# Moving an output projection's matmuls from the score part of each step into its softmax part

## The chip, the core and the metric

The kernel runs on one core of one Trainium2 chip. The metric is the device time of one execution in microseconds. Before the change it is 1201.21 us, the median of 3 runs (1199.9 to 1201.53).

The names used below: PE is the matrix engine (TensorE), DVE the vector engine, ACT the scalar engine, POOL is GpSimd, SP the engine whose queue issues most DMAs. Each engine runs its own instruction stream in order; they meet only at semaphores.

## The reference

One transformer block on `x` of 16 x 256 x 512 in float32: banded cross attention with rotary positions against a context of the same shape, then a quantised feed-forward layer.

```python
B, window = 128, 128                       # dk = 32, 16 heads
qp = _rope(einsum('bsd,ed->bse', layernorm(x), wq)); kp = _rope(einsum(..., ctx, wk)); vp = einsum(..., ctx, wv)
scores = einsum('bhnqd,bhnkd->bhnqk', qb, kband) * sqrt(dk)      # band of +-128 keys, rest masked
out = einsum('bhnqk,bhnkd->bhnqd', softmax(scores), vband)
x = x + (einsum('bsd,ed->bse', out, wo_w) + wo_b)
hidden = gelu(quantize_a16(layernorm(x)) @ quantize_w8(W_in) + b_in)
x = x + (quantize_a16(hidden) @ quantize_w8(W_out) + b_out)
```

## The kernel before, in words

The program has an attention phase (up to about 735 us of the span) and a feed-forward phase behind it. The change touches only the attention phase. It takes the 16 sequences one after the other, one step `b` for each sequence of 256 tokens, all 16 heads in a step. Matrix products whose operands need float32 accuracy are made of three products in the fp32r type: each operand is split into a leading part (`_hi`) and a rest (`_lo`), and hi x hi, hi x lo and lo x hi are summed.

A step is pipelined over three sequences. In step b the engines do the attention of sequence b, the projections (k, q, v) of sequence b + 1, and the output projection (`o_products`, with `wo`), residual and second layernorm's moments of sequence b - 1. Step 0 has no output projection (`has_o` is false), step 15 no projections (`has_proj` is false); steps 1 to 14 have both.

PE's order within a step is written out by hand in `step`:

- The score part. `scores(b, n)` makes the 256 x 256 scores of head n as two matmuls of 256 columns, into one of two banks of PSUM in turn (`ring`). DVE adds the mask and takes the row maxima (`row_maxima`, L1218, two instructions for a head); `scores` of head n may start only when the maxima of head n - 2 are done. Between the heads stand the projections of the next sequence: `tiles[n]` holds what PE does behind the scores of head n. The v projection of the second token half is 12 matmuls of 512 columns (`v_tile(b + 1, 1)`), 9 of them behind head 11 and 3 behind head 12.
- DVE's `split_max` (L1223 and L1225) then makes the negated maxima in two parts. PE transposes them (`max_transposes`, L617), ACT copies them into the stacked operand `q_st` (`max_copy`, L960), and SP spreads them to the other heads by three DMAs (`stack_max`, L352).
- The softmax part. `scores_t(b, n)` (L639) makes the transposed scores of head n with the maximum already subtracted, into three banks in turn; ACT takes the exponential (L967), POOL cuts the band (`band`, L1559). Behind heads 7, 11 and 15, and at the end, a `clump` of 32 narrow matmuls weighs v and sums the denominators of four heads.

The output projection of sequence b - 1 is 24 matmuls of 512 columns, 12 for each token half s, into `kv_bank[s]`. `o_products` is a generator: each `some(count)` in `step` issues the next `count` of them. Before the change 2 are issued behind head 14, 10 behind the last scores, 4 behind the transposes and 8 between the transposed scores. Within a half the 8 products with `t_hi` come first and the 4 with `t_lo` last, and the wait for `ot_lo` stands ahead of the latter. `t_hi` (ACT, `ot_lead`, L944) and `t_lo` (POOL, `ot_rest`, L1547) are the two parts of the normalised attention output; ACT's comes first, behind DVE's `normalise` (L1265), which stands behind head 9.

POOL's order in a step is: `split_lo` for k (L1536, four instructions), `ot_rest` twice, `bias_x` (L1552: adds the output bias to the residual's input `x_res`, two instructions, behind a wait for the DMA that loads `x_res`), then the first two quarters of `ctx_lo` (L1542), then the bands. DVE's `residual` (L1211) waits for the finished half (`o_mm`) and for `bias_x`. SP issues the load of `x_res` at the start of a step; in step 15 it first issues the loads of two tiles of the feed-forward phase's input (`load_xq`, 1 MB each).

## Time and profile before

| | |
|---|---|
| median of 3 runs | 1201.21 us |
| the profiled execution | 1201.21 us |
| its span, first to last instruction | 1199.5 us |
| PE busy | 1147.4 us (96%) |
| DVE busy | 953.4 us (79%) |
| ACT busy | 643.3 us (54%) |
| POOL busy | 373.3 us (31%) |
| granted PE clock, mean over the span | 0.987 |

The profiled execution took exactly the median, and 1.7 us of it lie outside the span. A busy PE is not a PE at its peak: its records overlap (the end of a matmul is modelled and lies behind the start of the next), so how fast PE goes is read from the distance between starts. In the timeline, "x4" is four merged instructions, and a bracket gives the engine's idle time before the row and what released it. The granted clock is 1.00 at 2.4 GHz and 0.50 at 1.2 GHz.

### The profile page before, as it was taken

To read this page: it belongs to the slowest core of one execution; us is meant where nothing else is said; L and a number is where in the kernel's file an instruction comes from. 1 tells how busy PE (TensorE), PEld (TensorE's weight loads), DVE (VectorE), ACT (ScalarE), POOL (GpSimd) and SP (SyncE) were. 2 spreads that over 40 slices of the span, in tenths; PEclk is the share of its full clock that TensorE was granted. 3 is DMA by queue.
4 is the path that set the end of the run, shared out by engine and by line. 5 is a ranking of instruction groups with operands and counts; after the bars stand their busy time and mean duration, and the time that the engine had idled before them with its cause. 6 is when DMAs were issued, how large, how long until landed. Compare 5 with 4: busy or idle time off the path is not lost.

```text
span 1199.5 us, 23540 instructions
## 1 busy us (share of the span) xinstructions
PE 1147.4 (96%) x7928; PEld 766.8 (64%) x7928; DVE 953.4 (79%) x2413; ACT 643.3 (54%) x1033; POOL 373.3 (31%) x540
## 2 busy tenths in 40 slices
PE   6989999999999999999999788999999999999998
PEld 6867877887787787788778555444444444444443
DVE  6769889989888988998898766666666688777776
ACT  6244355346435535634543454565655468777774
POOL 1146337436534733743563330000000021111121
PEclk9989999999999999999999889999999999999999
DMA  8454674574566458356545732555553402577662
GB/s 287 117 139 108 177 196 104 160 202 131 130 181 171 110 161 215 90 165 192 144 117 145 191 113 88 194 192 194 205 191 138 158 1 71 177 240 236 223 220 97
DMA packets 100522, 191.10 MB, mean 159 GB/s; under 512 B 13376, under 2 KB 30912, under 8 KB 100416
## 3 DMA queue, kind: packets, MB, share of 16 engines
q1 hardware_dynamic: 96096, 179.92, 49.7%
q10 hardware_dynamic: 4320, 9.83, 2.9%
q8 instruction: 59, 0.97, 0.3%
q14 instruction: 47, 0.39, 0.1%
HBM read 89.16 MB, written 43.91 MB: 111 GB/s over the span
## 4 chain that ended last, share of the span: by engine, by line
PE 47%; issue 24%; DVE 20%; DMA 5%; ACT 2%; SPq 1%; DVEq 0%; POOL 0%; POOLq 0%; ACTq 0%
PE bank L858 18%; DVE bank L1218 9%; PE bank L653 5%; PE bank L639 5%; PE bank L666 4%; DMA q_st<-q_st 3%; PE bank L515 3%; PE bank L514 3%; PE bank L516 3%; DVE row_max L1218 2%; PE bank L605 2%; DVE roped L1244 2%; DVE rt L1242 2%; DVE neg_max L1223 1%; DVE rt L1241 1%
## 5 line engine op out<-in xcount | busy, mean ns | idle before, releaser
L1218 DVE CUSTOM_DVE_ANT_0 bank<-bank,mask 128x256 f32<-128x256 f32 x512 | 202.7, 454 | 54.1 <-PE bank L605 44.5
L858 PE MATMUL bank<-wout_int,g_hi 128*128 128x512 bf16 x512 | 193.6, 379 | 0.1
L858 PE MATMUL bank<-wout_int,g_lo 128*128 128x512 bf16 x512 | 193.6, 379 | 0.0
L819 PE MATMUL bank<-qT_hi,win_int 128*128 128x512 bf16 x496 | 188.0, 379 | 0.0
L819 PE MATMUL bank<-qT_lo,win_int 128*128 128x512 bf16 x496 | 188.0, 379 | 0.0
L967 ACT ACTIVATE probs<-bank 128x512 f32<-128x512 f32 x256 | 135.7, 602 | 40.4 <-PE bank L639 38.8
L1536 POOL TENSOR_TENSOR k_lo<-roped,k_hi 128x256 fp32r<-128x256 f32 x60 | 55.2, 948 | 284.7 <-ACT k_hi L907 284.7
L1514 DVE TENSOR_TENSOR g_lo<-h_int,g_hi 128x512 f16<-128x512 f32 x128 | 89.1, 696 | 41.3 <-ACT g_hi L1123 37.4
L1559 POOL TENSOR_SCALAR_AFFINE_SELECT probs<-probs 128x256 f32<-128x256 f32 x256 | 107.0, 428 | 46.8 <-ACT probs L967 39.5
L639 PE MATMUL bank<-q_st,k_st 128*128 128x256 f32 x512 | 103.6, 302 | 11.4 <-DMA q_st<-q_st 6.0
L639 PEld LDWEIGHTS bank<-q_st,k_st 128*128 128x128 f32 x512 | 82.9, 192 | 44.4 <-issue 13.6
L1091 ACT ACTIVATE h_ring<-bank,b_in,g_scale 128x512 f32<-128x512 f32 x96 | 72.9, 778 | 71.4 <-PE bank L819 55.0
L1456 DVE TENSOR_REDUCE hmax<-h_ring 128x512 f32 (+1 forms) x96 | 63.1, 682 | 58.2 <-ACT h_ring L1091 56.3
L605 PE MATMUL bank<-k_st,q_st 96*128 96x256 f32 x512 | 96.8, 301 | 11.3 <-DVE row_max L1218 10.4
L1123 ACT CAST g_hi<-h_int 128x512 f16<-128x512 f32 x128 | 78.9, 617 | 47.2 <-PE bank L858 43.2
L605 PEld LDWEIGHTS bank<-k_st,q_st 96*128 96x128 f32 x512 | 77.5, 194 | 34.0 <-DVE row_max L1218 16.8
L1602 POOL TENSOR_TENSOR xq<-xq,b_out 128x512 f32<-128x512 f32 x32 | 41.5, 1296 | 166.5 <-ACT h_int L1132 166.5
L858 PEld LDWEIGHTS bank<-wout_int,g_hi 128*128 128x128 f16 x512 | 50.0, 98 | 60.9 <-issue 0.6
L858 PEld LDWEIGHTS bank<-wout_int,g_lo 128*128 128x128 f16 x512 | 50.1, 98 | 60.3 <-DVE g_lo L1514 0.2
L819 PEld LDWEIGHTS bank<-qT_hi,win_int 128*128 128x128 bf16 x496 | 48.5, 98 | 57.8 <-ACT h_ring L1091 0.3
L819 PEld LDWEIGHTS bank<-qT_lo,win_int 128*128 128x128 bf16 x496 | 48.5, 98 | 57.7
L1132 ACT ACTIVATE h_int<-h_ring,magic_c,tiny 128x512 f32<-128x512 f32 x96 | 77.9, 812 | 0.0
(170 smaller groups left out, 2678.4 us busy)
## 6 DMA issues: line engine op xcount, KB each, us to landing
hidden_scratch<-h_ring SPq DMA_DIRECT2D x96, 256.0 KB, 2.1
h_ring<-hidden_scratch SPq DMA_DIRECT2D x96, 256.0 KB, 2.8
k_st<-k_hi SPq DMA_DIRECT2D x128, 128.0 KB, 2.6
q_st<-q_hi SPq DMA_DIRECT2D x128, 128.0 KB, 2.6
xq<-x_scratch SPq DMA_DIRECT2D x16, 1024.0 KB, 6.1
x_ln<-in_x SPq DMA_DIRECT2D x16, 512.0 KB, 6.4
ctx_raw<-in_ctxT SPq DMA_DIRECT2D x16, 512.0 KB, 5.1
k_st<-k_lo SPq DMA_DIRECT2D x64, 128.0 KB, 2.7
```

The costliest lines, as they stand in the source:

```text
L605: mm = pe.matmul(ring[n % 2][:, qb * S:(qb + 1) * S], q_st[0:MROW, n, qb * P:(qb + 1) * P], k_st[0:MROW, n], start=True, stop=True)
L639: mm = pe.matmul(third[n][:, kb * S:(kb + 1) * S], k_st[:, n, kb * P:(kb + 1) * P], q_st[:, n], start=True, stop=True)
L819: mm = pe.matmul(bank[f % 4][:], win_int[:, c, f * P:(f + 1) * P], part[:, par, c], start=c == 0 and part is qT_hi, stop=c == KC - 1 and p ...
L858: return pe.matmul(bank[4 * par + u][:], part[:, f % 4, u * P:(u + 1) * P], wout_int[:, f], start=f == 0 and part is g_hi, stop=f == FC - ...
L967: act.activation(probs[:, n % SLOTS].rearrange("p k q -> p (k q)"), third[n][:], ACT.Exp, scale=SCORE_SCALE).then_inc(exp_done, 1)
L1091: act.activation(dst, bank[f % 4][:], ACT.Gelu, bias=b_in[:, f:f + 1], scale=g_scale[:, f:f + 1]).then_inc(gelu_done, 1)
L1123: act.copy(g_hi[:, f % 4], h_int[:, f % 4]).then_inc(ghi_done, 1)
L1132: act.activation(h_int[:, f % 4], chunk, ACT.Identity, bias=magic_c[:], scale=tiny[:, 5:6]).then_inc(hint_done, 1)
L1218: dve.tensor_tensor_reduce(sc, sc, mask[:, (1 - qb) * P:(1 - qb) * P + S], 1.0, NEG, ALU.add, ALU.max, row_max[:, qb, n:n + 1]).then_inc(m ...
L1456: dve.tensor_reduce(hmax[:, bass.ds(FC * n + f, 1)], src, AX_X, ALU.max, apply_absolute_value=True).then_inc(hmax_done, 1)
L1514: dve.tensor_tensor(g_lo[:, f % 4], h_int[:, f % 4], g_hi[:, f % 4], ALU.subtract).then_inc(glo_done, 1)
L1559: pool.affine_select(out=far, in_=far, compare_op=ALU.is_ge, fill=0.0, base=1 - P, pattern=[[0, 2], [1, P]], channel_multiplier=1).then_in ...
```

## The change

PE's o products of a step now stand 4 ahead of the transposes (10 + 2 before), 4 behind them (as before) and 16 between the transposed scores (8 before). Each product triple goes hi x hi, hi x lo, lo x hi within one chunk, so the wait for `ot_lo` of a half now stands ahead of its first product. The v projection's second half is cut 6 + 6, behind heads 11 and 13, instead of 9 + 3 behind heads 11 and 12. On POOL, `bias_x` stands ahead of `ot_rest`.

```diff
--- before.py
+++ after.py
@@ -575,6 +575,7 @@
                 for s in range(2):
                     tok = slice(s * P, (s + 1) * P)
                     pe.wait_ge(ot_hi, 2 * j + s + 1)
+                    pe.wait_ge(ot_lo, 2 * j + s + 1)
                     if s == 0:
                         pe.wait_ge(w_lo_done, 5)
                     if has_proj:
@@ -582,15 +583,13 @@
                     else:
                         pe.wait_ge(res_done, 2 * j)
                     for c in range(KC):
-                        for w in (w_hi, w_lo):
-                            pe.matmul(kv_bank[s][:], t_hi[:, c, tok], w["wo"][:, c], start=c == 0 and w is w_hi, stop=False)
+                        parts = ((t_hi, "hi"), (t_hi, "lo"), (t_lo, "hi"))
+                        for m, (part, w) in enumerate(parts):
+                            mm = pe.matmul(kv_bank[s][:], part[:, c, tok], (w_hi if w == "hi" else w_lo)["wo"][:, c],
+                                           start=c == 0 and m == 0, stop=c == KC - 1 and m == 2)
+                            if c == KC - 1 and m == 2:
+                                mm.then_inc(o_mm, 1)
                             yield
-                    pe.wait_ge(ot_lo, 2 * j + s + 1)
-                    for c in range(KC):
-                        mm = pe.matmul(kv_bank[s][:], t_lo[:, c, tok], w_hi["wo"][:, c], start=False, stop=c == KC - 1)
-                        if c == KC - 1:
-                            mm.then_inc(o_mm, 1)
-                        yield
 
             def scores(b, n):
 
@@ -718,32 +717,32 @@
 
             def step(b, par, has_c, has_o, has_proj, has_xt):
 
-                tiles = [[] for _ in range(H)]
+                tiles = [[] for _ in range(H // 2)]
+                if has_proj:
+                    tiles[0] += [lambda: qk_tile(b + 1, "k", 0)]
+                    tiles[1] += [lambda: x_transposes(b + 1, 0), lambda: x_transposes(b + 1, 1), lambda: qk_tile(b + 1, "k", 1)]
+                    tiles[2] += [lambda: v_tile(b + 1, 0)]
+                    tiles[3] += [lambda: qk_tile(b + 1, "q", 0)]
+                    tiles[4] += [lambda: qk_tile(b + 1, "q", 1)]
+                    tiles[5] += [lambda: v_tile(b + 1, 1, range(2))]
+                    tiles[6] += [lambda: v_tile(b + 1, 1, range(2, KC))]
+                for n in range(H):
+                    scores(b, n)
+                    if n % 2:
+                        for tile in tiles[n // 2]:
+                            tile()
+
+
                 heavy = o_products(b - 1, has_proj) if has_o else iter(())
 
                 def some(count):
                     for _ in range(count):
                         next(heavy, None)
 
-                if has_proj:
-                    tiles[1] += [lambda: qk_tile(b + 1, "k", 0)]
-                    tiles[3] += [lambda: x_transposes(b + 1, 0), lambda: x_transposes(b + 1, 1), lambda: qk_tile(b + 1, "k", 1)]
-                    tiles[5] += [lambda: v_tile(b + 1, 0)]
-                    tiles[7] += [lambda: qk_tile(b + 1, "q", 0)]
-                    tiles[9] += [lambda: qk_tile(b + 1, "q", 1)]
-                    tiles[11] += [lambda: v_tile(b + 1, 1, range(3))]
-                    tiles[12] += [lambda: v_tile(b + 1, 1, range(3, KC))]
-                tiles[14] += [lambda: some(2)]
-                for n in range(H):
-                    scores(b, n)
-                    for tile in tiles[n]:
-                        tile()
-
-
-                some(10)
+                some(4)
                 max_transposes(b, has_proj)
                 some(4)
-                for n, count in enumerate((1, 1, 1, 1, 1, 1, 1, 0, 1, 0, 0, 0, 0, 0, 0, 0)):
+                for n, count in enumerate((1, 2, 2, 3, 1, 1, 1, 0, 1, 1, 1, 0, 1, 1, 0, 0)):
                     scores_t(b, n, has_o, has_proj)
                     some(count)
                     if n in (7, 11, 15):
@@ -1569,9 +1568,10 @@
                     for c in range(KC):
                         split_lo("k", b + 1, c)
                 if has_o:
+                    bias_x(b - 1)
+                if has_o:
                     ot_rest(b - 1, 0)
                     ot_rest(b - 1, 1)
-                    bias_x(b - 1)
                 if has_xt:
                     ctx_lo(b + 2, 0)
                     ctx_lo(b + 2, 1)
```

The places on PE and POOL in step 1 (steps 2 to 14 are alike). First PE's tail of the score part. L605 (L604 after) are the scores, two matmuls for a head; L514 to L516 the v projection; L586 and L590 (L588 after) the o products; L617 (L616 after) the transposes of the maxima. Before, from the scores of head 12 on, where the two heads 13 and 14 are one row of four:

```order
L605 MATMUL bank<-k_st,q_st 128x256 x2
L514 MATMUL bank<-wv_hi,cT_hi 128x512
L515 MATMUL bank<-wv_lo,cT_hi 128x512
L516 MATMUL bank<-wv_hi,cT_lo 128x512
L605 MATMUL bank<-k_st,q_st 128x256 x4
L586 MATMUL bank<-wo_hi,t_hi 128x512
L586 MATMUL bank<-wo_lo,t_hi 128x512
L605 MATMUL bank<-k_st,q_st 128x256 x2
```

After, from the six v matmuls that now stand behind head 13 (the first row is heads 12 and 13, the last heads 14 and 15):

```order
L604 MATMUL bank<-k_st,q_st 128x256 x4
L514 MATMUL bank<-wv_hi,cT_hi 128x512
L515 MATMUL bank<-wv_lo,cT_hi 128x512
L516 MATMUL bank<-wv_hi,cT_lo 128x512
L514 MATMUL bank<-wv_hi,cT_hi 128x512
L515 MATMUL bank<-wv_lo,cT_hi 128x512
L516 MATMUL bank<-wv_hi,cT_lo 128x512
L604 MATMUL bank<-k_st,q_st 128x256 x4
```

Three of the nine v matmuls behind head 11 have moved behind head 13, and the two o products between heads 14 and 15 are gone.

PE ahead of the transposes, before, from the last scores on:

```order
L605 MATMUL bank<-k_st,q_st 128x256 x2
L586 MATMUL bank<-wo_hi,t_hi 128x512
L586 MATMUL bank<-wo_lo,t_hi 128x512
L586 MATMUL bank<-wo_hi,t_hi 128x512
L586 MATMUL bank<-wo_lo,t_hi 128x512
L586 MATMUL bank<-wo_hi,t_hi 128x512
L586 MATMUL bank<-wo_lo,t_hi 128x512
L590 MATMUL bank<-wo_hi,t_lo 128x512 x4
L617 MATMUL bank<-ident,neg_max 128x128 x2
```

After:

```order
L604 MATMUL bank<-k_st,q_st 128x256 x4
L588 MATMUL bank<-wo_hi,t_hi 128x512
L588 MATMUL bank<-wo_lo,t_hi 128x512
L588 MATMUL bank<-wo_hi,t_lo 128x512
L588 MATMUL bank<-wo_hi,t_hi 128x512
L616 MATMUL bank<-ident,neg_max 128x128 x2
```

Ten products between the last scores and the transposes have become four, and the third of the four already reads `t_lo`.

PE between the transposed scores of heads 0 to 4, before (L639 are the transposed scores):

```order
L639 MATMUL bank<-q_st,k_st 128x256 x2
L586 MATMUL bank<-wo_hi,t_hi 128x512
L639 MATMUL bank<-q_st,k_st 128x256 x2
L586 MATMUL bank<-wo_lo,t_hi 128x512
L639 MATMUL bank<-q_st,k_st 128x256 x2
L586 MATMUL bank<-wo_hi,t_hi 128x512
L639 MATMUL bank<-q_st,k_st 128x256 x2
L586 MATMUL bank<-wo_lo,t_hi 128x512
L639 MATMUL bank<-q_st,k_st 128x256 x2
```

After (L638 are the transposed scores):

```order
L638 MATMUL bank<-q_st,k_st 128x256 x2
L588 MATMUL bank<-wo_hi,t_lo 128x512
L638 MATMUL bank<-q_st,k_st 128x256 x2
L588 MATMUL bank<-wo_hi,t_hi 128x512
L588 MATMUL bank<-wo_lo,t_hi 128x512
L638 MATMUL bank<-q_st,k_st 128x256 x2
L588 MATMUL bank<-wo_hi,t_lo 128x512
L588 MATMUL bank<-wo_hi,t_hi 128x512
L638 MATMUL bank<-q_st,k_st 128x256 x2
L588 MATMUL bank<-wo_lo,t_hi 128x512
L588 MATMUL bank<-wo_hi,t_lo 128x512
L588 MATMUL bank<-wo_hi,t_hi 128x512
```

Eight products stand here instead of four. Four more have moved behind heads 8 to 13.

POOL in step 1, before:

```order
L1536 TENSOR_TENSOR k_lo<-roped,k_hi 128x256 x4
L1547 TENSOR_TENSOR t_lo<-oT,t_hi 128x4x128 x2
L1552 TENSOR_TENSOR x_res<-x_res,wo_b 128x512 x2
L1542 TENSOR_TENSOR cT_lo<-ctx_raw,cT_hi 128x256 x2
L1559 AFFINE_SELECT probs<-probs 128x256 x2
```

After:

```order
L1535 TENSOR_TENSOR k_lo<-roped,k_hi 128x256 x4
L1551 TENSOR_TENSOR x_res<-x_res,wo_b 128x512 x2
L1546 TENSOR_TENSOR t_lo<-oT,t_hi 128x4x128 x2
L1541 TENSOR_TENSOR cT_lo<-ctx_raw,cT_hi 128x256 x2
L1558 AFFINE_SELECT probs<-probs 128x256 x2
```

The two instructions that write `x_res` and the two that write `t_lo` have changed places.

## Rows read from the trace of the kernel before

**Rows 1.** List of waits, whole span: engine, line waited for, total us, times, longest
```profile
PE bank L617 <- DVE neg_max L1225: 10.5, 15, 1.6
```

**Rows 2.** Timeline, PE, end of a steady step's score part: start us, us, instruction
```profile
313.95 0.40 PE L605 MATMUL bank<-k_st,q_st 96*128 96x256 f32 x2
...
314.89 0.40 PE L605 MATMUL bank<-k_st,q_st 96*128 96x256 f32 x2
315.56 0.51 PE L605 MATMUL bank<-k_st,q_st 96*128 96x256 f32 x2 [0.27 <-DVE row_max L1218]
...
316.41 0.50 PE L605 MATMUL bank<-k_st,q_st 96*128 96x256 f32 x2
...
318.14 1.09 PE L590 MATMUL bank<-wo_hi,t_lo 128*128 128x512 f32 x4
319.91 0.44 PE L617 MATMUL bank<-ident,neg_max 128*128 128x128 f32 x2 [0.68 <-DVE neg_max L1225]
...
320.89 0.40 PE L586 MATMUL bank<-wo_lo,t_hi 128*128 128x512 f32 x1
321.13 0.39 PE L639 MATMUL bank<-q_st,k_st 128*128 128x256 f32 x2
```

**Rows 3.** Timeline, DVE, the same stretch
```profile
313.49 0.13 DVE L1218 DVE_READ_ACCUMULATOR2_ANT row_max<- 128x1 f32 x1
...
314.54 0.43 DVE L1218 CUSTOM_DVE_ANT_0 bank<-bank,mask 128x256 f32<-128x256 f32 x1
...
318.01 1.15 DVE L1223 TENSOR_SCALAR neg_max<-row_max 128x32 fp32r<-128x32 f32 x1
319.20 0.66 DVE L1225 SCALAR_TENSOR_TENSOR neg_max<-row_max,neg_max 128x32 fp32r<-128x32 f32 x1
```

**Rows 4.** Timeline, POOL, the same stretch
```profile
314.10 2.54 POOL L1547 TENSOR_TENSOR t_lo<-oT,t_hi 128x512 fp32r<-128x512 f32 x2
316.61 2.52 POOL L1552 TENSOR_TENSOR x_res<-x_res,wo_b 128x512 f32<-128x512 f32 x2
319.09 1.41 POOL L1542 TENSOR_TENSOR cT_lo<-ctx_raw,cT_hi 128x256 fp32r<-128x256 f32 x2
```

**Rows 5.** One line's instructions, L1223 and L1225: ns min/median/max, first and last start
```profile
L1223 DVE TENSOR_SCALAR neg_max<-row_max x16: 181/1172/1187, 61.0 to 695.7; 128x32 fp32r<-128x32 f32 x16
...
L1225 DVE SCALAR_TENSOR_TENSOR neg_max<-row_max,neg_max x16: 192/656/658, 61.2 to 695.9; 128x32 fp32r<-128x32 f32 x16
```

**Rows 6.** Timeline, PE, the same step's transposed part and the next step's start
```profile
323.46 0.51 PE L639 MATMUL bank<-q_st,k_st 128*128 128x256 f32 x2 [0.30 <-DMA q_st<-q_st]
...
325.30 1.07 PE L653 MATMUL bank<-probs,v_sb 128*32 128x256 f32 x16
...
327.17 0.51 PE L639 MATMUL bank<-q_st,k_st 128*128 128x256 f32 x2
...
331.85 0.50 PE L639 MATMUL bank<-q_st,k_st 128*128 128x256 f32 x2 [0.22 <-ACT probs L967]
...
336.34 0.74 PE L605 MATMUL bank<-k_st,q_st 96*128 96x256 f32 x4
```

**Rows 7.** Timeline, PE, the last step (15): its first row and its transposes
```profile
676.06 0.74 PE L605 MATMUL bank<-k_st,q_st 96*128 96x256 f32 x4
...
697.84 0.38 PE L617 MATMUL bank<-ident,neg_max 128*128 128x128 f32 x2
```

**Rows 8.** Timeline, POOL, the last step
```profile
690.43 2.50 POOL L1547 TENSOR_TENSOR t_lo<-oT,t_hi 128x512 fp32r<-128x512 f32 x2 [16.88 <-ACT t_hi L944]
696.58 2.53 POOL L1552 TENSOR_TENSOR x_res<-x_res,wo_b 128x512 f32<-128x512 f32 x2 [3.65 <-DMA x_res<-in_x]
```

**Rows 9.** Busy time by stretch: length, busy of each engine, granted clock, DMA
```profile
58.50:61.90 3.40, 1.37 (x6) 0.72 (x6) 3.33 (x16) 1.07 (x3) 1.41 (x2) 1.00 0.00 0
61.97:72.00 10.03, 8.03 (x48) 5.09 (x48) 8.16 (x17) 6.07 (x11) 6.55 (x12) 0.50 0.52 119
318.00:321.40 3.40, 2.72 (x15) 1.90 (x14) 3.32 (x5) 1.01 (x2) 2.50 (x3) 1.00 0.00 0
```

## The prediction

> **What bounds the kernel now.** I read the busy shares first: PE is busy 96% of the span, DVE 79%. Then the list of waits, for what stops PE in the attention phase: the transposes of the maxima wait for DVE's L1225 in 15 of the 16 steps [rows 1]. Then the timelines of one steady step, engine by engine, where the change sits. The scores of heads 0 and 1 of the next step start at 336.34, those of step 15 at 676.06, eight steps later [rows 6, 7]: a steady step takes (676.06 - 336.34) / 8 = 42.5 us.
>
> In that step PE has two regimes. From the scores of head 12 at 313.95 to the transposes at 319.91 it follows DVE: head 14 waits 0.27 us for the maxima of head 12, and behind the last o product of the twelve PE waits again 0.68 us, for L1225 [rows 2]. From the transposed scores at 321.13 to the next step's scores at 336.34 it is 15.21 us of nearly dense work, with stops that are small: 0.30 for the DMA that spreads the maxima, 0.22 for an exponential [rows 2, 6].
>
> What ends the first regime is not DVE's arithmetic. L1223 takes 0.18 us in its shortest case and 1.17 in the median; L1225 0.19 and 0.66 [rows 5]. In the steady step L1223 starts at 318.01 and ends at 319.16, and POOL's fourth instruction of the rest and bias pairs ends at 316.61 + 2.52 = 319.13; L1225 then ends at 319.86, and the first of POOL's two `ctx_lo` instructions ends near 319.09 + 1.41 / 2 = 319.8 [rows 3, 4]. So each of them lasts until the POOL instruction that it met is over, and the transposes' time is set by POOL's row of work.
>
> **The v projection's cut, 6 + 6.** A 512 column product is 0.24 us from start to start (320.89 to 321.13) [rows 2]. Three fewer ahead of head 12 let its scores start up to 0.7 us sooner, at 313.25, but they need the maxima of head 10, which DVE has at 313.49 + 0.13 = 313.62 [rows 2, 3]; they start near 313.68. Head 13 then waits for the maxima of head 11, near 314.4. Behind it stand six v matmuls instead of two score heads: 314.44 + 0.34 (the longer start after a wait, 315.56 to the next matmul) + 6 x 0.235 = 316.2 for head 14, 0.6 later than the 315.56 of before; head 15 follows at 316.4, as before. DVE got to head 12 0.59 us behind its scores (313.95 to 314.54) and needs 0.77 for a head, so its last maxima end near 318.3 instead of 317.9, 0.4 later. L1223 then starts at 318.4, still within the POOL instruction that ends at 319.13, and ends when it did. I take 0 for the cut. If L1223's length were its own, it would be +0.4 a step, 14 x 0.4 = 5.6 us.
>
> The Trainium skill, in GPSIMD Engine Reference (Specifications), says that GpSimd's SBUF interfaces are shared with VectorE, with contention for DVE instructions in a two-port mode or with two SBUF inputs. By it L1225, with two inputs in SBUF, is such a one, and the 0.4 is swallowed; by the instruction's duration alone 5.6 us would be added. The trace agrees with the page (0.18 against 1.17 us).
>
> **The wait for `ot_lo` and POOL's new order.** The four instructions are 1.27 and 1.26 us each and only change places [rows 4]: bias to 316.61, rest of half 0 to 317.9, of half 1 to 319.13. PE's first o product needs half 0 now: with the last scores out at 316.7 it stops until 317.9, does four products (until 319.0) and stops again until 319.91. Queued behind the first stop are these four and the transposes, which aren't ready anyway. 0 us.
>
> **Eight o products moved behind the transposes.** This is the term. Before, ten stood between the last scores and the transposes and two between heads 14 and 15; of those twelve four remain. PE's idle time ahead of the transposes grows by what they were, 8 x 0.235 = 1.9 us, and they come back in the dense part. Walked through: from 321.13 to the transposed scores of head 4 stand 4 heads and 8 products, 12 x 0.235 = 2.8, so 323.95 instead of 323.46, since the DMA's 0.30 stop and the slower start behind it go: +0.5 for four more products. To the first clump three heads with products and one without, as before, without the start after a stop: +0.4 there (325.30 before). The second quarter had 1.62 us (327.17 to the next clump) with one product and a stop for exponentials; three products fit into 0.1 + 7 x 0.235 = 1.7: +0.1. The third quarter has two more products but its 0.22 stop goes, and its head 15 waits for the exponential of head 12 whatever stands between: 0 [rows 6]. Sum 0.45 a step, and 14 x 0.45 = 6.3 us. The ends: all stops of before swallow it (0), or none do (14 x 1.9 = 26 us); I stay with the walk, because its stops are in the rows. DVE's residual of half 0 comes at 323.9, half 0's last product at 322.8; half 1's is done near 332.4, the residual at 332.9: no new wait, with 0.5 us to spare.
>
> **Step 0** has no o products; the score cut lets DVE end about 0.4 us sooner, with POOL idle: -0.4 us.
>
> **Step 15.** Here the swap on POOL costs. `t_lo` was made at 690.43 to 692.9, and `bias_x` started only at 696.58, when the load of `x_res` had landed behind two loads of 1 MB [rows 8]. With the bias ahead, `t_lo` of half 0 comes at 696.58 + 2.53 + 1.26 = 700.4, and PE, in order, has its four products and then the transposes behind that wait. PE runs at half clock there (it has been idle most of the step), so the four take 4 x 0.47 = 1.9 us, and the transposes are at 702.3 instead of 697.84 [rows 7]: +4.4. The products behind them start at half clock too, some 4 of them, +0.9; the extra ones behind head 8 vanish between exponentials. Taken +5.5. The bounds: if `x_res` lands ahead of 690, the step gains some 1.5 us (six products fewer ahead of transposes whose maxima are ready); if the half clock lasts through the step's softmax part, +9.
>
> **The clock.** The granted clock fell to 0.50 (1.2 GHz) in step 0, behind 3.4 us in which PE was busy 1.37, and stayed there 10 us; in the steady step, with 2.72 of 3.4 us busy across the transposes, it stayed at 1.00 [rows 9]. After the change PE stands idle 1.1 + 0.8 us around four products there, so it is busy about 1.5 of 3.4. That is nearer to the stretch that fell. But step 0 had a sparse softmax part behind it, and here the work behind is dense, so a fall should last some 3.4 us rather than 10 and cost half of that, 1.6 us with the stops gone. No row shows how many steps would fall: between 0 and 14, so 0 to 22 us. I take two, +3, nearer to the row of 1.00 in every steady step, because the average of PE's work over a step hardly moves.
>
> The Trainium skill, in TensorE: Matmul & The Clock Gate (A second HAM failure mode), says that micro-idles between groups of matmuls can make the clock swing between its two levels. By it all 14 steps are in danger; the row of step 0 agrees that a fall behind a sparse stretch happens here, and no row shows it within a steady step.
>
> **The sum.** 1201.2 + 6.3 - 0.4 + 5.5 + 3 = 1215.6, so 1216 us. It starts from the profiled execution's 1201.21, which is the median. A measurement of this kernel tells about 0.2% (2.4 us) from no change.
>
> **The rivals.**
>
> 1. The clock falls in most steady steps. For it: 1.5 of 3.4 us busy is close to the 1.37 that fell. Against it: the dense work on both sides. 14 x 1.6 = 22 instead of 3: 1235 us; with half the steps 1224.
> 2. Only the dense term and a small step 15. For it: step 15's `x_res` is one DMA, with a landing time that could differ by some us, and the clock may not fall. 1201.2 + 6.3 - 0.4 + 0 to 2: 1207 to 1209 us.
> 3. The softmax part swallows all: if ACT's exponentials and not PE set its pace, the eight products cost nothing, as PE's stops there for ACT and the DMA add up with the slow starts behind them to about 1.5 of the 1.9 us; with step 15's gain or loss of up to 2, 1200 to 1203 us: no change. Against it: two of three clumps start behind dense PE rows.
> 4. Faster. ACT makes `cT_hi` only behind the copy of the later v half, so POOL's `ctx_lo` could start later than 319.13. Then L1225 meets an idle POOL and takes 0.19 instead of 0.66, and the transposes come 0.47 sooner in 13 steps: -6.1 us. It decides if `cT_hi` is over 1 us later than I reckon (318.1, the v half 1.3 us later than before). With the softmax part swallowing the products and step 15 at -1.5, 1201.2 - 6.1 - 0.4 - 1.5 = 1193 us; with the dense term it comes out at 1199 and without step 15's gain at no change. It needs three things that I reckon otherwise.
> 5. DVE is later than reckoned and misses POOL's fourth instruction, meeting both `ctx_lo` ones: +0.7 in 13 steps, 1225 us. It has 0.7 us to spare.
>
> **How the numbers follow.** The forecast (two or so falls, step 15 at 4 to 7): 0.45, with 1211 to 1221 as its own range. Rival 1: 0.15. Rival 2: 0.15. Rival 3: 0.10. Rival 4: 0.06. Rival 5: 0.09. The range 1205 to 1229 leaves out rivals 3 and 4 and the upper end of rival 1, together about 0.2. Faster by over 0.2%: 0.05 (most of rival 4). Within 0.2%: 0.10. Slower by over 0.2%: 0.85.
>
> **What would show it.** In a steady step: L1223 still over 0.7 us long and ending with a POOL instruction; the transposes still 5.9 to 6 us behind 313.95's place in the step; PE idle about 1.1 us until POOL's `t_lo` and 0.8 us until L1225; the distance between steps 42.9 instead of 42.5 where the clock is 1.00; the stop for the DMA ahead of head 4 gone. In step 15: PE waiting for POOL's `t_lo`, which stands behind the load of `x_res`, to about 700 plus the shift. The granted clock across the transposes tells rival 1 from the rest. The forecast is wrong if the step distance stays at 42.5, if a steady step stands at 0.50 in most steps, or if step 15's `x_res` lands before its `t_hi`.

## The result and the profile after

| | before | after |
|---|---|---|
| median | 1200.92 us (4 runs, 1199.9 to 1201.53) | 1221.79 us (4 runs, 1219.11 to 1223.11) |
| the profiled execution | 1201.21 us | 1221.89 us |
| its span | 1199.5 us | 1220.0 us |
| PE busy | 1147.4 us | 1146.5 us |
| granted PE clock, mean | 0.987 | 0.977 |

The change makes the kernel slower: the ratio is 1.0172 [1.0152, 1.0192], 20.5 us more in the span. The forecast was 1216, with 1205 to 1229 as its range.

Two distances cut every step of the trace at the same places. The score part runs from the first scores to the transposes of the maxima, the softmax part from these to the next step's first scores. Before, they are 26.1 and 16.4 us in each steady step (steps 1 to 14; the score part of step 14 is 25.6, before and after). After, the score part is 26.05. The softmax part is 17.01 to 17.03 in seven steps (1, 2, 7, 8, 9, 13, 14) and 18.44 to 18.56 in the other seven (3 to 6, 10 to 12).

PE's timeline in step 9, one of the first kind, answers to [rows 2, 6]:

```profile
452.11 0.63 PE L604 MATMUL bank<-k_st,q_st 96*128 96x256 f32 x4
453.84 0.47 PE L588 MATMUL bank<-wo_hi,t_hi 128*128 128x512 f32 x1 [1.09 <-issue]
...
455.78 0.44 PE L616 MATMUL bank<-ident,neg_max 128*128 128x128 f32 x2 [0.77 <-DVE neg_max L1224]
...
459.80 0.39 PE L638 MATMUL bank<-q_st,k_st 128*128 128x256 f32 x2
...
461.52 1.07 PE L652 MATMUL bank<-probs,v_sb 128*32 128x256 f32 x16
...
463.39 0.51 PE L638 MATMUL bank<-q_st,k_st 128*128 128x256 f32 x2
...
465.25 1.07 PE L652 MATMUL bank<-probs,v_sb 128*32 128x256 f32 x16
...
472.79 0.74 PE L604 MATMUL bank<-k_st,q_st 96*128 96x256 f32 x4
```

The two idle stretches around the four o products are there, 1.09 and 0.77 us. The first is put down to "issue", but it ends with POOL's first rest, 452.47 + 1.26 = 453.73 in the next fence. From the transposes the transposed scores of head 4 are 459.80 - 455.78 = 4.02 us away (3.55 before), the first clump 5.74 (5.39), the second 9.47 (8.88), the next step 17.01 (16.43). The stop of 0.30 for the DMA ahead of head 4 is gone.

DVE and then POOL in the same step, answering to [rows 3, 4]:

```profile
454.37 0.66 DVE L1222 TENSOR_SCALAR neg_max<-row_max 128x32 fp32r<-128x32 f32 x1
455.06 0.66 DVE L1224 SCALAR_TENSOR_TENSOR neg_max<-row_max,neg_max 128x32 fp32r<-128x32 f32 x1
```

```profile
449.99 2.52 POOL L1551 TENSOR_TENSOR x_res<-x_res,wo_b 128x512 f32<-128x512 f32 x2
452.47 2.52 POOL L1546 TENSOR_TENSOR t_lo<-oT,t_hi 128x512 fp32r<-128x512 f32 x2
454.96 1.41 POOL L1541 TENSOR_TENSOR cT_lo<-ctx_raw,cT_hi 128x256 fp32r<-128x256 f32 x2
```

DVE's last maxima end 1.41 us ahead of the transposes instead of 1.90 (319.91 - 318.01), so DVE is 0.49 later. L1222 (L1223 before) nevertheless ends where POOL's fourth instruction does, 455.03 against 454.99: it is only shorter, 0.66 instead of 1.15.

Now step 6, one of the seven long ones. PE's timeline:

```profile
323.19 0.47 PE L588 MATMUL bank<-wo_hi,t_hi 128*128 128x512 f32 x1 [1.11 <-issue]
...
325.13 0.69 PE L616 MATMUL bank<-ident,neg_max 128*128 128x128 f32 x2 [0.77 <-DVE neg_max L1224]
325.47 0.78 PE L588 MATMUL bank<-wo_lo,t_hi 128*128 128x512 f32 x1
326.05 0.63 PE L588 MATMUL bank<-wo_hi,t_lo 128*128 128x512 f32 x1
326.47 0.63 PE L588 MATMUL bank<-wo_hi,t_hi 128*128 128x512 f32 x1
```

And busy time by stretch (length, busy time of each engine with its instructions, granted clock, DMA), for step 9, step 6 twice, and step 0 twice; it answers to [rows 9]:

```profile
454.00:457.40 3.40, 2.63 (x13) 1.85 (x13) 3.30 (x7) 1.06 (x2) 2.37 (x3) 1.00 0.00 0
323.30:326.70 3.40, 2.63 (x9) 1.92 (x10) 3.30 (x7) 0.84 (x2) 2.41 (x3) 0.74 0.00 0
325.50:328.20 2.70, 2.70 (x10) 2.22 (x9) 2.63 (x5) 1.27 (x3) 0.21 (x1) 0.50 0.13 31
61.97:68.50 6.53, 5.66 (x29) 4.31 (x32) 6.00 (x12) 5.59 (x11) 4.10 (x9) 0.51 0.52 120
68.50:79.00 10.50, 10.07 (x141) 5.74 (x132) 4.13 (x11) 6.01 (x15) 6.82 (x14) 0.98 0.53 118
```

Steps 6 and 9 have the same instructions and the same idle time. In step 6 the granted clock is 0.50 (1.2 GHz) from the transposes to 328.3 (the row below), the products come 0.42 to 0.43 us apart instead of 0.235, and the softmax part is 1.4 us longer. In step 0 the clock is back at about 68.9 instead of 72.2.

```profile
324.91:328.32 3.41, 3.19 (x10) 2.71 (x11) 3.34 (x6) 1.39 (x3) 0.80 (x2) 0.50 0.14 32
```

In step 15 POOL and then PE answer to [rows 8] and [rows 7]:

```profile
711.20 2.48 POOL L1551 TENSOR_TENSOR x_res<-x_res,wo_b 128x512 f32<-128x512 f32 x2 [21.60 <-DMA x_res<-in_x]
713.65 2.49 POOL L1546 TENSOR_TENSOR t_lo<-oT,t_hi 128x512 fp32r<-128x512 f32 x2
```

```profile
708.20 1.56 PE L604 MATMUL bank<-k_st,q_st 96*128 96x256 f32 x4 [0.42 <-DVE row_max L1217]
715.00 0.76 PE L588 MATMUL bank<-wo_hi,t_hi 128*128 128x512 f32 x1 [5.24 <-issue]
...
716.85 0.63 PE L616 MATMUL bank<-ident,neg_max 128*128 128x128 f32 x2
```

PE stands idle for 5.24 us until `t_lo`, which stands behind the load of `x_res`. The score part of step 15 is 24.74 us instead of 21.78.

The account of the 20.5 us of span, by these distances: the softmax parts without a fallen clock 14 x 0.58 = 8.1; the seven falls of the clock 7 x 1.51 = 10.6 (by their mean softmax part, 18.52 against 17.01); the score parts -0.5; step 0 -2.1 (score part +0.2, softmax part 17.54 instead of 19.85); step 15 +3.0 up to the transposes and +2.2 behind them; the rest, -0.8, lies in the feed-forward phase (-0.7) and in rounding.

### The profile page after: what moved, and what is told of

It reads as the page before. It is cut to its first block, busy times and chain, and to the rows that moved or that the text cites. A ratio compares the mean times of both kernels' runs of the same rounds, so it can differ in the third digit from the quotient of the medians.

```text
span 1220.0 us, 23511 instructions
## 1 busy us (share of the span) xinstructions
PE 1146.5 (94%) x7884; PEld 775.4 (64%) x7928; DVE 946.9 (78%) x2413; ACT 646.5 (53%) x1033; POOL 372.9 (31%) x540
## 4 chain that ended last, share of the span: by engine, by line
PE 55%; issue 24%; DVE 17%; DMA 2%; SPq 1%; ACT 1%; DVEq 0%; POOL 0%; POOLq 0%
PE bank L857 18%; DVE bank L1217 7%; PE bank L588 7%; PE bank L638 6%; PE bank L652 5%; PE bank L665 4%; PE bank L604 3%; PE bank L514 3%; PE bank L515 3%; PE bank L516 3%; DVE row_max L1217 2%; DVE roped L1243 2%; DVE rt L1241 1%; DVE rt L1240 1%; PE bank L529 1%
## 5 line engine op out<-in xcount | busy, mean ns | idle before, releaser
L857 PE MATMUL bank<-wout_int,g_hi 128*128 128x512 bf16 x491 | 185.8, 379 | 0.3 <-issue 0.2
L818 PE MATMUL bank<-qT_hi,win_int 128*128 128x512 bf16 x474 | 179.6, 379 | 0.0
L966 ACT ACTIVATE probs<-bank 128x512 f32<-128x512 f32 x256 | 139.9, 600 | 53.2 <-PE bank L638 49.7
L638 PEld LDWEIGHTS bank<-q_st,k_st 128*128 128x128 f32 x512 | 95.8, 201 | 30.5 <-issue 13.2
L638 PE MATMUL bank<-q_st,k_st 128*128 128x256 f32 x512 | 107.3, 301 | 2.0 <-ACT probs L966 1.1
L604 PE MATMUL bank<-k_st,q_st 96*128 96x256 f32 x512 | 94.0, 300 | 15.8 <-DVE row_max L1217 14.8
L604 PEld LDWEIGHTS bank<-k_st,q_st 96*128 96x128 f32 x512 | 75.3, 194 | 37.1 <-issue 23.4
L947 ACT COPY v_sb<-bank 128x512 f32<-128x512 f32 x32 | 18.8, 586 | 121.2 <-PE bank L516 121.2
```

What stands on the lines that cost most here:

```text
L604: mm = pe.matmul(ring[n % 2][:, qb * S:(qb + 1) * S], q_st[0:MROW, n, qb * P:(qb + 1) * P], k_st[0:MROW, n], start=True, stop=True)
L638: mm = pe.matmul(third[n][:, kb * S:(kb + 1) * S], k_st[:, n, kb * P:(kb + 1) * P], q_st[:, n], start=True, stop=True)
L818: mm = pe.matmul(bank[f % 4][:], win_int[:, c, f * P:(f + 1) * P], part[:, par, c], start=c == 0 and part is qT_hi, stop=c == KC - 1 and p ...
L857: return pe.matmul(bank[4 * par + u][:], part[:, f % 4, u * P:(u + 1) * P], wout_int[:, f], start=f == 0 and part is g_hi, stop=f == FC - ...
L966: act.activation(probs[:, n % SLOTS].rearrange("p k q -> p (k q)"), third[n][:], ACT.Exp, scale=SCORE_SCALE).then_inc(exp_done, 1)
```

## The experiments

Theory A: the loss is three terms, the moved products (some 8 us), falls of the granted clock behind the sparse stretch (some 10), and step 15's swap on POOL (some 5). Theory B: one term, the sparse stretch or the swap, makes nearly all of it. Ratios are against runs of the kernel before on the same chip.

### POOL's order alone (pool_swap)

```diff
                 if has_o:
+                    bias_x(b - 1)
                     ot_rest(b - 1, 0)
                     ot_rest(b - 1, 1)
-                    bias_x(b - 1)
```

> The kernel before with POOL's order alone changed: bias_x ahead of ot_rest. Theory (the swap costs only in the last step): steady steps stay 42.5 us apart, the granted clock stays at 1.00 in them, and in step 15 the transposes come about 5 us later, since POOL's t_lo stands behind the load of x_res: 1206 us (+5). Rival (the swap also delays t_lo in every step, and the o products with it): t_lo of half 0 comes at the place of 317.9 instead of 315.4, and if the first half's lo products then wait, the transposes move by 0.3 us in 14 steps: 1210. Rival (the swap costs nothing): 1201.

Measured: 1204.86 us, ratio 1.0032 [1.0018, 1.0046]. The steady parts are 26.1 and 16.4 as before, in all but step 11, whose softmax part is 17.73. That is no fall, the clock is 1.00 there: ahead of head 4 PE waits for the DMA that spreads the maxima, 1.60 us instead of 0.30.

```profile
536.85 0.50 PE L639 MATMUL bank<-q_st,k_st 128*128 128x256 f32 x2 [1.60 <-DMA q_st<-q_st]
```

Step 15's score part is 26.18 instead of 21.78, +4.4. POOL and then PE there:

```profile
697.36 2.48 POOL L1552 TENSOR_TENSOR x_res<-x_res,wo_b 128x512 f32<-128x512 f32 x2 [23.06 <-DMA x_res<-in_x]
699.80 2.49 POOL L1547 TENSOR_TENSOR t_lo<-oT,t_hi 128x512 fp32r<-128x512 f32 x2
```

```profile
701.12 2.07 PE L590 MATMUL bank<-wo_hi,t_lo 128*128 128x512 f32 x4 [4.27 <-POOL t_lo L1547]
702.99 0.63 PE L617 MATMUL bank<-ident,neg_max 128*128 128x128 f32 x2
```

Here the profile names the releaser that "issue" hid in the changed kernel. The swap costs nothing in a steady step and +4.4 in step 15 up to the transposes. Behind them step 15 is 1.0 us longer too, though no product has moved: the clock is at 0.50 for another 3.5 us.

### The v projection's cut alone (v_cut)

```diff
-                    tiles[11] += [lambda: v_tile(b + 1, 1, range(3))]
-                    tiles[12] += [lambda: v_tile(b + 1, 1, range(3, KC))]
+                    tiles[11] += [lambda: v_tile(b + 1, 1, range(2))]
+                    tiles[13] += [lambda: v_tile(b + 1, 1, range(2, KC))]
```

> The kernel before with the v projection's second half cut 6 + 6 behind heads 11 and 13 instead of 9 + 3 behind heads 11 and 12. Theory (L1223 lasts until the POOL instruction that it meets is over, and swallows DVE's later end): L1223 starts about 0.4 us later and is about 0.7 instead of 1.15 us long, the score part stays 26.1 us, 1201 us give or take 1. Rival (DVE's time alone): score part +0.4 us in 14 steps, 1207 us.

Measured: 1200.18 us, ratio 0.9991 [0.9977, 1.0005]; parts 26.07 and 16.43. One line's instructions (ns minimum, median, maximum):

```profile
L1223 DVE TENSOR_SCALAR neg_max<-row_max x16: 182/694/703, 62.5 to 695.2; 128x32 fp32r<-128x32 f32 x16
```

The median is 694 ns instead of 1172 [rows 5]: DVE comes 0.48 us later and ends when it did. The cut costs nothing.

### The o products' counts alone (counts_only)

The kernel before with 4 | 4 | 16 instead of 12 | 4 | 8; the order within a half, the v cut and POOL are as before.

```diff
-                tiles[14] += [lambda: some(2)]
...
-                some(10)
+                some(4)
                 max_transposes(b, has_proj)
                 some(4)
-                for n, count in enumerate((1, 1, 1, 1, 1, 1, 1, 0, 1, 0, 0, 0, 0, 0, 0, 0)):
+                for n, count in enumerate((1, 2, 2, 3, 1, 1, 1, 0, 1, 1, 1, 0, 1, 1, 0, 0)):
```

> The kernel before with the o products' places alone changed: 4 ahead of the transposes, 4 behind, 16 among the transposed scores; the order of the products within a half, the v cut and POOL stay as before. Theory (PE's idle time ahead of the transposes moves 8 products into the dense part, and the sparse stretch lets the clock fall in some steps): softmax part 17.0 instead of 16.4 us in steps at 1.00, about 18.6 in 4 to 10 steps at 0.50, step 15 about 1 us shorter: 1213 us, between 1209 and 1221. Rival (the clock falls because of the products' order or POOL's order): no falls, 1208 us. Rival (the products are free, and the changed kernel's loss is from elsewhere): 1201.

Measured: 1226.04 us, ratio 1.0214 [1.0186, 1.0242]: a miss, and slower than the whole change. Step 1 has a softmax part of 17.02, the 13 behind it 18.3 to 18.5. PE at the transposes of step 8:

```profile
416.35 0.69 PE L617 MATMUL bank<-ident,neg_max 128*128 128x128 f32 x2 [2.08 <-DVE neg_max L1224]
```

The products' term is as in the changed kernel (0.58 a step, from step 1, the only one without a fall), but the clock falls in 13 of 14 steps. So the falls need neither the new order of the products nor POOL's. Two neighbouring falls, steps 7 and 8, by busy time in their stretches:

```profile
371.43:374.85 3.42, 2.91 (x9) 2.53 (x10) 3.35 (x6) 1.12 (x3) 1.09 (x2) 0.50 0.07 16
415.81:419.22 3.41, 2.87 (x9) 2.49 (x10) 3.34 (x6) 1.07 (x3) 1.11 (x2) 0.50 0.06 14
```

PE is idle in one stretch of 2.08 us here, since nothing stops its four products on the way. Step 15's score part is 18.91, 2.9 less than before: its maxima don't wait behind twelve slow products.

### The changed kernel with POOL's order of before (after_pool_back)

The reverse of the first diff, in the changed kernel.

> The changed kernel with POOL's order put back (ot_rest ahead of bias_x). Theory (the swap costs 5 us in step 15 and nothing else): step 15's transposes come within 1 us of DVE's L1224 instead of 5.6 us behind it, the softmax parts of the other steps stay 17.0 at 1.00 and 18.6 at 0.50, 1216 us if as many steps fall as in the changed kernel (7); the idle time ahead of the transposes is then one stretch of 2 us instead of two of 1.1 and 0.8. Rival (the two stretches make the fall): fewer than 3 falls, 1209 us. Rival (the swap costs nothing): 1221.

Measured: 1222.63 us, ratio 1.0177 [1.0149, 1.0205]: a miss. Step 15's score part is 19.20, 5.5 less than in the changed kernel, as expected; but ten steps have a softmax part of 18.4 to 18.6. PE in step 8:

```profile
417.10 0.44 PE L616 MATMUL bank<-ident,neg_max 128*128 128x128 f32 x2 [2.09 <-DVE neg_max L1224]
```

So the swap on POOL costs 5.5 us in step 15, and the profile with it has three falls fewer, 7 against 10, which is 4.5 us; the softmax part of step 0 differs by another 1.4 (17.54 against 18.93). That falls become fewer because the swap cuts the idle time in two fits all four profiles (7 and 4 falls with two stretches, 13 and 10 with one), but four profiles are few for it, since the count varies from run to run. I had overlooked it.

### PE's idle time filled (after_fill)

The changed kernel with 12 extra matmuls of 256 columns, in bf16 and into a bank that nobody reads then, in the two idle stretches; the output isn't touched. The wait keeps them off the bank until the v half in it has been copied.

```diff
+                if has_proj and has_o:
+                    pe.wait_ge(v_done, 2 * (b + 2) - 1)
+                    keep_busy(bank[6], 7)
                 some(4)
+                if has_proj and has_o:
+                    keep_busy(bank[6], 5)
                 max_transposes(b, has_proj)
```

> The changed kernel with PE's idle time ahead of the transposes filled in steps 1 to 14: 7 matmuls of zeros and weights, 256 columns each, ahead of the four o products and 5 behind them, into a bank that nothing reads before it is written anew (extra work, the rest unchanged). Theory (sparse work ahead of the transposes makes the clock fall): no steady step at 0.50, all softmax parts 17.0 us instead of 18.5 in 7 of them, 1211 us (-11). Rival (the fall comes from what follows the transposes or from the average of a step): still 4 or more falls, 1217 or more. Rival (the filler itself delays the transposes): score parts over 26.3 us.

Measured: 1214.13 us, ratio 1.0112 [1.0084, 1.0140]. All steady softmax parts are 17.00 to 17.04, with no fall, and the score parts 26.05. The total is 3 us above the 1211 expected. PE in step 8:

```profile
404.80 0.94 PE L691 MATMUL bank<-win_int 128*128 128x256 bf16 x7
406.08 0.47 PE L588 MATMUL bank<-wo_hi,t_hi 128*128 128x512 f32 x1 [0.34 <-issue]
...
407.09 0.72 PE L691 MATMUL bank<-win_int 128*128 128x256 bf16 x5
408.02 0.44 PE L616 MATMUL bank<-ident,neg_max 128*128 128x128 f32 x2 [0.21 <-DVE neg_max L1229]
```

The instructions that matter stand where they stood, only the idle time has shrunk, and 7.7 us are gone. (The five lines added ahead of it make L1224 to L1229.) This shows the falls as a term of their own, and that PE's idle time brings them about.

### The same with POOL's order of before (fill_back)

As the last two together, with 16 extra matmuls in one piece behind `some(4)`.

> The changed kernel with POOL's order put back and the idle 2.1 us ahead of the transposes filled by 16 matmuls of 256 columns in steps 1 to 14, so that of the change only the moved products and the v cut are left. Theory (the loss is the sum of moved products, falls and step 15's wait): softmax parts 17.0 us and none at 0.50, step 15's transposes as in after_pool_back, so 14 x 0.55 = 8 us over the kernel before: 1208 us. Rival (the order of the products or the split waits cost by themselves): 1212 or more.

Measured: 1208.03 us, ratio 1.0070 [1.0049, 1.0092]. No fall, softmax parts 17.01 to 17.03, step 15's score part 19.16. What is left of the loss, 7 us by the medians, is the moved products' 8.1, with step 15 at -2.6 ahead of its transposes and +1.9 behind them, and a small rest in the ends. That is theory A: three terms, of which none makes nearly all of the loss. In ratios, filling is worth 0.0060 x 1201 = 7.2 us in the changed kernel and 0.0107 x 1201 = 12.9 with POOL's old order. Each of these two is uncertain by some 4 us; at 1.5 a fall they would be 5 and 8 or 9 falls, where the profiles have 7 and 10.

### The changed kernel once more (after_again)

> The changed kernel once more, unchanged, for a second profile. Theory (where the clock falls depends on the moment that a sparse stretch meets): again about 7 falls, perhaps not in the same steps; the softmax parts are 17.0 or 18.5 and the score parts 26.05. Rival (the 7 were an accident of one execution): 0 to 3 or 11 to 14.

Measured: 1219.01 us, a single execution. The softmax part is 18.39 to 18.55 in steps 2, 6, 7, 8, the four with a fall. In step 11 it is 17.61 at a clock of 1.00, where PE stops ahead of head 4 for the DMA of the maxima, 0.32 us. So the run has 4 falls, where about 7 were expected. Which steps fall differs from run to run, though the instructions and idle times are alike (1.12 and 0.76 us in step 9 here, which stayed at 1.00). Step 0's softmax part is 18.44 us instead of 17.54, as the clock came back later.

### POOL quiet under the negated maxima (quiet, after_quiet)

The kernel before, in which POOL waits for `split_max` ahead of `bias_x`, and by its order ahead of `ctx_lo` and the bands. Then the same edit in the changed kernel.

```diff
                     ot_rest(b - 1, 0)
                     ot_rest(b - 1, 1)
+                    if has_xt or has_proj:
+                        pool.wait_ge(msplit, 2 * (b + 1))
                     bias_x(b - 1)
```

> The kernel before with bias_x and all of POOL behind it held back in steps 1 to 14 until split_max's two instructions are done. Theory (L1223 and L1225 are long only because a POOL instruction runs): L1223 and L1225 about 0.2 us each, the transposes 0.8 us sooner, bounded then by PE's twelve o products, the score part 25.3 instead of 26.1 us; 14 x 0.8 = 11 us less, 1190 us. Rival (POOL, held back, makes the bands late): the softmax part grows by 0.5 or more and takes it back, 1197 to 1201. Rival (the long L1223 is its own): 1201 or more.

Measured: 1203.37 us, ratio 1.0016 [1.0003, 1.0030], so not the 1190 expected but above even the rival's 1197 to 1201. The two DVE instructions and, below, PE in step 8:

```profile
L1223 DVE TENSOR_SCALAR neg_max<-row_max x16: 180/181/182, 61.6 to 696.7; 128x32 fp32r<-128x32 f32 x16
...
L1225 DVE SCALAR_TENSOR_TENSOR neg_max<-row_max,neg_max x16: 191/193/194, 61.9 to 696.9; 128x32 fp32r<-128x32 f32 x16
```

```profile
411.04 1.07 PE L653 MATMUL bank<-probs,v_sb 128*32 128x256 f32 x16 [1.06 <-POOL probs L1559]
```

The mechanism of DVE's wait holds: with POOL quiet they take 0.18 and 0.19 us instead of 1.17 and 0.66, and the score part is 25.25, 0.84 shorter. But POOL is late by what it waited, and the first clump stops 1.06 us for its bands: the softmax part is 17.49, 1.06 longer.

> The changed kernel with POOL's ot_rest first and bias_x and what follows held back until split_max is done, in steps 1 to 14. Theory: the transposes come 1.1 us sooner (score part 24.95 instead of 26.05), the idle time ahead of them is about 1 us instead of 1.9, so the clock falls in at most 2 steps, and step 15 is 2 to 5 us shorter: 1222 - 15 - 10 - 2 = 1195 us, faster than the kernel before by 0.5%. Rival (falls depend on the moved products and not on the idle time): 7 or more falls, 1206.

Measured: 1209.51 us, ratio 1.0074 [1.0046, 1.0102]: a miss by POOL's lateness again (softmax parts 18.3, score parts 25.08). The clock stayed at 1.00 in all steady steps, so the rival fails, by which the moved products and not the idle time bring the falls. PE in step 8:

```profile
407.82 0.44 PE L616 MATMUL bank<-ident,neg_max 128*128 128x128 f32 x2 [1.15 <-DVE neg_max L1224]
```

### POOL quiet, its work put elsewhere, two products moved (quiet8)

The kernel before with that wait, all four quarters of `ctx_lo` behind bands 1, 3, 11 and 13, and two o products moved behind the transposes.

```diff
+                    if has_xt or has_proj:
+                        pool.wait_ge(msplit, 2 * (b + 1))
...
-                    ctx_lo(b + 2, 0)
-                    ctx_lo(b + 2, 1)
...
-                    if n in (1, 3) and has_xt:
-                        ctx_lo(b + 2, n // 2 + 2)
+                    if n in (1, 3, 11, 13) and has_xt:
+                        ctx_lo(b + 2, (1, 3, 11, 13).index(n))
...
-                some(10)
+                some(8)
...
-                for n, count in enumerate((1, 1, 1, 1, 1, 1, 1, 0, 1, 0, 0, 0, 0, 0, 0, 0)):
+                for n, count in enumerate((1, 1, 1, 2, 1, 1, 1, 0, 1, 1, 0, 0, 0, 0, 0, 0)):
```

> A candidate for a faster kernel: the kernel before, bias_x held back until split_max is done, ctx_lo's first quarters moved behind bands 1 and 3 and the others behind bands 11 and 13, and two of the ten o products ahead of the transposes moved behind heads 3 and 9. Theory: the transposes come when DVE is done (score part 24.8 to 25.0), the softmax part grows by 0.2 at most, no falls: 1201.2 - 14 x 1.0 = 1187 us. Rival (PE's own work bounds the step, so the moved products come back in full): as quiet alone, 1190.

Measured: 1189.21 us, ratio 0.9908 [0.9879, 0.9936], faster than both kernels. The score part is 24.78 and the softmax part 17.0, 41.8 us a step instead of 42.5. PE at the transposes of step 8:

```profile
396.41 0.63 PE L590 MATMUL bank<-wo_hi,t_lo 128*128 128x512 f32 x2
396.88 0.38 PE L617 MATMUL bank<-ident,neg_max 128*128 128x128 f32 x2
397.01 0.72 PE L590 MATMUL bank<-wo_hi,t_lo 128*128 128x512 f32 x2
```

PE no longer stops ahead of the transposes. In `quiet` it didn't either: there the twelve products set the transposes' time, and with two fewer the score part is 0.47 us shorter (25.25 to 24.78), 2 x 0.235. So moving products behind them pays here, since the maxima are ready sooner and no idle time takes the products' place. The softmax part grew by 0.57, not by the 0.2 at most that was expected, so the total lies nearer to the rival's 1190 than to the theory's 1187, though not for the rival's reason. Only 0.14 of it stands ahead of the third clump, where the two products are. The rest comes ahead of the last one, where PE waits for POOL's late bands:

```profile
412.01 1.07 PE L653 MATMUL bank<-probs,v_sb 128*32 128x256 f32 x16 [0.36 <-POOL probs L1559]
```

## Why the prediction was right, and where not

The direction and the terms were right. The sum came 5.8 us short of the measured median because the falls were counted too low: they cost 10.6 us in the profiled run instead of 3. That it came so near is in part luck, since step 0 gave back 1.7 us more than reckoned, for a reason that isn't the change's. The measured 1221.8 lies in the range 1205 to 1229, but just outside the 1211 to 1221 that the forecast proper (two falls or so) had.

1. **v cut and L1223: right.** 0 was taken against 5.6; measured -1.3 us within an interval that holds 0. DVE came 0.49 later (0.4 reckoned) and L1223 swallowed it. One reading there was loose: 0.18 against 1.17 us is L1223's, with one input in SBUF, and not that of the instruction with two, L1225, which takes 0.19 against 0.66. In which mode L1223 ran no trace shows.
2. **The wait for `ot_lo` in a steady step: right for the path, incomplete for the clock.** Both stops came, 1.09 and 0.77 (1.1 and 0.8 reckoned), and the transposes kept their place. That two stretches may bring fewer falls than one wasn't in the working.
3. **Eight products: mechanism right, size 0.58 instead of 0.45**, 8.1 us instead of 6.3. To head 4 it was +0.47 (0.5 reckoned), to the first clump +0.35 (0.4), in the second quarter +0.24 (0.1), in the third 0.
4. **Step 0: -2.1 instead of -0.4.** DVE's earlier end didn't show (the score part is 0.2 longer); the gain is the clock's, back at 1.00 some 3.3 us sooner. In kernels whose step 0 differs as little as those tried here, its softmax part ranged from 17.45 to 19.85 us, and in two profiles of the changed kernel it was 17.54 and 18.44. So this term can't be forecast to 2 us, and the gain isn't the change's.
5. **Step 15: +5.5 reckoned, +5.2 measured** (3.0 and 2.2). It is right in sum, while the parts differ: the swap alone costs 4.4 to 5.5, and fewer products at half clock ahead of the transposes give 2.6 back (21.78 to 19.20 with POOL's old order). The 2.2 behind them aren't the products' alone: the clock stays at 0.50 for 4 us more there, and in `pool_swap`, without moved products, 3.5 us of it cost 1.0.
6. **The clock: the step that failed in size.** Two falls were taken, seven came in the profiled run and four in the second profile; length and price of one were right, 3.4 us and 1.5 on average against 3.4 and 1.6. The argument that "the average of PE's work over a step hardly moves" was what failed. PE has the same matmuls in a steady step of both kernels, and none of the 14 steps fell before. `after_fill` adds matmuls only in the idle stretches, 1.7 us of a step's 43, and had no fall.

Of the rivals, the first (falls in most or half of the steps) was the nearest: with half the steps, as in the profiled run, its 1224 is 2 us off and the forecast 6. The sign of being wrong (a steady step at 0.50 in most steps) stopped just short of coming: seven of fourteen. Rival 2, no falls, is what `after_fill` shows: 1214, not 1207 to 1209, as the products and the step 15 term are larger than it had them. Rival 3 failed, as the softmax part didn't swallow the products. Rival 4 failed, as `ctx_lo` started at 454.96, right behind the fourth instruction; its mechanism was real, and `quiet8` used it. Rival 5 failed, as DVE met the fourth instruction with 0.6 us to spare.

Not settled: why of two steps with the same instructions and idle times one falls and the other doesn't. The clock records of the four profiles with falls in steady steps (34 in all) show two things. Each fall begins between 0.54 us before and 0.94 us behind a step's transposes, and where two neighbouring steps fall, the falls begin 44.4 us apart, in every case (415.81 - 371.43 above is one). In `counts_only` a step with a fall is itself 44.4 us long, so each fall meets the next step at the same place, and 13 come in a row. In the changed kernel it is 44.5 to 44.6, the place moves by some 0.2 us a step, and its rows of falls ended after one to four. So the moment at which the clock falls looks as if it weren't tied to the step; no run moved the steps against it, and this stays an inference.

## What to carry to other kernels

Moving work off an engine ahead of its wait for another engine leaves a hole there and puts the work into the dense part: it pays only where that part has slack, or where the wait ends sooner as well, so that the engine still has no hole there. Before making a dense matrix engine idle for a microsecond or two in each step, look at whether the granted clock stays at 1.00, since the hole can cost more than the work that was moved. A tiny instruction that takes a different time in different places of a trace isn't bound by its own work: look at what runs on the neighbouring engine when it ends.

## What the runs showed of the hardware

- **A short idle stretch can cost the clock, and its form counts.** Profiled steady steps with a softmax part lengthened by a clock at 0.50: with one idle stretch of 2.1 us ahead of the transposes 13 and 10 of 14; with 1.1 and 0.8 around four products 7, and in a second run 4; with 1.15 alone, or with extra matmuls in the stretches, 0. A fall lasted 3.4 us and cost 1.3 to 1.5. The Trainium skill, in TensorE: Matmul & The Clock Gate (A second HAM failure mode), tells of a kernel that cycles its PSUM queue, in which micro-idles between groups of matmuls make the clock swing. These runs agree that idle stretches so short can do it, here one or two in each step of 43 us. Its section What's actually happening says that how many matmuls run at the lower clock at a kernel's start varies from run to run of the same kernel. The two profiles of the changed kernel differ in the same way further in (17.54 and 18.44 us in step 0, falls in other steps).
- **DVE's small SBUF instructions wait for POOL's running one to end.** A 128x32 instruction took 0.18 us beside an idle POOL, 0.69 and 1.17 beside its 128x512 additions, depending on when it met them. The Trainium skill, in GPSIMD Engine Reference (Specifications), names the shared interface; `quiet` shows its price, 0.84 us of a step's score part.
- **The reverse, smaller.** POOL's two `bias_x` instructions took 2.52 us under the small ones [rows 4] and 3.0 beside DVE's rotary instructions (`rt`, `roped`) in `quiet` and `quiet8`.
